# A graph network's last pass: the chunk softmax's pieces put two to a step, and the summing of a group moved from 32 to 26 steps behind its gathers

## What is computed

```
h = x @ W[r];  s = h @ a_src[r];  d = h @ a_dst[r]          # per relation r
e = leaky_relu(s[src] + d[dst], 0.2), only edges of type r and a loop at each node
alpha = exp(e - max over edges with the same dst) / sum of the same
out = x @ W_self + b_self + sum over r of (segment_sum(alpha * h[src]) + bias[r])
```

## Time and profile before

| | us |
|---|---|
| median of 3 runs | 8430.0 (8417.5 to 8430.58) |
| the profiled execution's own time | 8409.43 |
| its span, first to last instruction | 8407.5 |
| POOL busy | 5989.0 (71%) |
| PE busy | 3614.6 (43%) |
| DVE busy | 3113.7 (37%) |
| ACT busy | 1009.6 (12%) |

### The profile page before, as it was taken

One profiled execution on the slowest core, in us unless ns is written; L12 is line 12 of the kernel. 1 busy time (PEld: TensorE's weight loads), 2 busy tenths in 40 slices (PEclk: granted clock), 3 DMA queues, 4 the chain that ended last, 5 costly groups with the idle time before them and its releaser, 6 DMA issues.

```text
span 8407.5 us, 78987 instructions
## 1 busy us (share of the span) xinstructions
PE 3614.6 (43%) x14426; PEld 2885.7 (34%) x14427; DVE 3113.7 (37%) x5678; ACT 1009.6 (12%) x3308; POOL 5989.0 (71%) x6283
## 2 busy tenths in 40 slices
PE   3444333333344434444344343434512555555555
PEld 3333333332222222222222222222312454555555
DVE  3323232323223232323222222222444566666666
ACT  0000000000000000000000000000200233333335
POOL 7777777776777777776777777777267777777770
PEclk6566565555665656566565655656655666666667
DMA  2111111111222222222111111111444554554553
GB/s 58 31 30 30 30 30 30 30 30 42 54 56 57 55 58 55 58 55 48 28 29 28 29 28 29 28 29 28 136 112 102 125 141 128 138 132 129 139 139 86
DMA packets 575401, 546.64 MB, mean 65 GB/s; under 512 B 344667, under 2 KB 344667, under 8 KB 575008
## 3 DMA queue, kind: packets, MB, share of 16 engines
q0 software_dynamic: 200704, 212.34, 13.8%
q1 hardware_dynamic: 345920, 271.71, 11.7%
q10 hardware_dynamic: 28384, 58.61, 1.9%
HBM read 440.61 MB, written 100.74 MB: 64 GB/s over the span
## 4 chain that ended last, share of the span: by engine, by line
POOL 56%; issue 24%; DVE 8%; PE 4%; DVEq 3%; DMA 2%; ACT 1%; POOLq 1%; ACTq 0%; SPq 0%
POOL gat L776 56%; PE p_b L1388 2%; DVEq L331 1%; DMA trip<-in_type_w 1%; ACT msg L989 1%; DVE sel L2031 1%; DVE sel L2035 1%; PE p_a L1449 1%; PE p_a L1447 1%; DVE oh L1668 0%; PE p_all L1377 0%; DVE oht L2027 0%; DVE sum_t L2063 0%; DVE dtab L2128 0%; ACT spare L1036 0%
## 5 line engine op out<-in xcount | busy, mean ns | idle before, releaser
L776 POOL DMA_INDIRECT gat<-x_d,idx x3136 | 2966.3, 946 | 1018.0 <-issue 1018.0
L776 POOL DMA_INDIRECT gat<-rel_d,idx x1568 | 1535.3, 979 | 685.7 <-issue 632.6
L776 POOL DMA_INDIRECT gat<-in_x,idx x1568 | 1485.5, 947 | 486.7 <-issue 486.7
L1668 DVE SCALAR_TENSOR_TENSOR oh<-dstf,fine_col,p_b 128x512 f32<-128x512 f32 x1578 | 1107.3, 743 | 381.9 <-issue 342.5
L1251 PE MATMUL p_all<-oh,gat 128*128 128x256 f32 x1568 | 720.6, 640 | 1194.6 <-DMA gat<-x_d,idx 1153.6
L1251 PE MATMUL p_all<-oh,msg 128*128 128x256 f32 x1568 | 714.5, 635 | 1183.4 <-DVE oh L1668 1183.4
L1237 PE MATMUL p_all<-oh,msg 128*66 128x128 f32 x3136 | 703.1, 417 | 1188.4 <-DVE oh L1668 1188.4
L1237 PEld LDWEIGHTS p_all<-oh,msg 128*66 128x66 f32 x3136 | 637.8, 230 | 1251.7 <-issue 1096.0
L1251 PEld LDWEIGHTS p_all<-oh,gat 128*128 128x128 f32 x1568 | 488.9, 327 | 1423.9 <-issue 1115.5
L1251 PEld LDWEIGHTS p_all<-oh,msg 128*128 128x128 f32 x1568 | 486.1, 325 | 1399.8 <-issue 1080.4
L1388 PE MATMUL p_b<-oh,msg 128*72 128x128 f32 x3136 | 664.7, 400 | 81.5 <-ACT msg L989 35.8
(11 more groups left out here) (275 smaller groups left out, 3344.1 us busy)
## 6 DMA issues: line engine op xcount, KB each, us to landing
he_d<-gat ACTq DMA_DIRECT2D x196, 288.0 KB
ea<-he_d SPq DMA_DIRECT2D x196, 288.0 KB
ea<-in_edge_attr SPq DMA_DIRECT2D x196, 256.0 KB, 2.7
gat<-x_d,idx POOLq DMA_INDIRECT x3136
drow<-dst_d SPq DMA_DIRECT2D x196, 256.0 KB
spare<-rel_d SPq DMA_DIRECT2D x98, 288.0 KB
gat<-in_x,idx POOLq DMA_INDIRECT x1568
gat<-rel_d,idx POOLq DMA_INDIRECT x1568
```

The costliest lines, as they stand in the source:

```text
L776: nc.gpsimd.indirect_dma_start(out=gat[:, q, s, :] if width == HROW else got[:, q, s, :], out_offset=None, in_=table, in_offset=bass.Indir ...
L1668: return vec.scalar_tensor_tensor(out=oh[:, u, cut, :], in0=bc(dst.unsqueeze(2), P, S // 2, W), scalar=fine_col[0:P, bass.ds(at, 1)], in1= ...
```

## The change

LAG goes from 32 to 26, READY from 48 to 46 and LAST from 246 to 244. The pieces of the softmax stand at other steps of the chunk:

| piece | engine | j before | j after |
|---|---|---|---|
| near (loads) | SP | 2 | 0 |
| widen | DVE | 1 | 1 |
| others | DVE | 3 | 2 |
| lay_scores, evict_scores | PE, ACT | 3, 4 | 2, 3 |
| own_scores, lay_self | DVE, PE | 5, 5 | 4, 4 |
| own_self, with_self | DVE | 6 | 5 |
| breaks, most_so_far | DVE | 7, 8 | 6, 6 |
| most_of_all, gaps | DVE | 9, 10 | 7, 7 |
| factors, exponents | DVE, ACT | 11, 11 | 8, 8 |
| sum_so_far, back_exponents | DVE, PE | 12, 12 | 9, 9 |
| sum_of_all, own_sums | DVE | 13, 0 of the next chunk | 10, 10 |
| back_sums | PE | 1 of the next chunk | 11 |
| weights | DVE | 2 of the next chunk, after the look | 12, before the look |
| chunk_shares | DVE | 4 of the next chunk, before the look | 12, before the look |

```diff
-LAG = 2 * CH + 4
+LAG = 2 * CH - 2
-READY = LAG + CH + SETTLE
+READY = LAG + CH + SETTLE + 4
...
-                if j == 2 and CH <= lo < G + CH:
+                if j == 0 and CH <= lo < G + CH:
...
-                    for at, piece in ((4, evict_scores), (11, exponents)):
+                    for at, piece in ((3, evict_scores), (8, exponents)):
...
-                if j == 1 and 2 * CH <= lo < G + 2 * CH:
-                    back_sums(k - 1)
...
-                    for at, piece in ((3, lay_scores), (5, lay_self), (12, back_exponents)):
+                    for at, piece in ((2, lay_scores), (4, lay_self), (9, back_exponents), (11, back_sums)):
...
+                k, j = chunk_of(it, i)
+                if CH <= lo < G + CH and j == LAG - CH:
+                    weights(k)
...
-                    for at_step, piece in ((0, own_sums), (2, weights)):
-                        if j == at_step:
-                            piece(k - 1)
                 if CH <= lo < G + CH:
-                    pieces = {1: (widen,), 3: (others,), 5: (own_scores,), 6: (own_self, with_self), 7: (breaks,),
-                              8: (most_so_far,), 9: (most_of_all,), 10: (gaps,), 11: (factors,), 12: (sum_so_far,),
-                              13: (sum_of_all,)}
+                    pieces = {1: (widen,), 2: (others,), 4: (own_scores,), 5: (own_self, with_self), 6: (breaks, most_so_far),
+                              7: (most_of_all, gaps), 8: (factors,), 9: (sum_so_far,), 10: (sum_of_all, own_sums)}
```

More of the change, by code:

```diff
@@ L2225, in look_share_and_scan @@
                     ahead()
-                k, j = chunk_of(it, i)
-                if 2 * CH <= lo < G + 2 * CH:
-                    for at_step, piece in ((0, own_sums), (2, weights)):
-                        if j == at_step:
-                            piece(k - 1)
                 if CH <= lo < G + CH:
-                    pieces = {1: (widen,), 3: (others,), 5: (own_scores,), 6: (own_self, with_self), 7: (breaks,),
-                              8: (most_so_far,), 9: (most_of_all,), 10: (gaps,), 11: (factors,), 12: (sum_so_far,),
-                              13: (sum_of_all,)}
+                    pieces = {1: (widen,), 2: (others,), 4: (own_scores,), 5: (own_self, with_self), 6: (breaks, most_so_far),
+                              7: (most_of_all, gaps), 8: (factors,), 9: (sum_so_far,), 10: (sum_of_all, own_sums)}
                     for piece in pieces.get(j, ()):
```

## The result

| | before | after |
|---|---|---|
| median of the runs made together, us | 8426.5 (4) | 8478.8 (4), 8476.7 to 8480.4 |
| ratio to before, 95% interval | | 1.0063 [1.0051, 1.0075] |
| span of the profiled execution | 8407.5 | 8474.8 |
| one chunk's round (steps 56 to 168, by 8) | 149.1 | 156.8 |
| last gather to the end | 227.3 | 211.6 |

The change makes the kernel 0.63% slower, 52 us. I had forecast 8450, slower by 0.25%, in the range 8408 to 8482: the direction and both halves of the account came, the size was less than half. The measured time lies only 3 us under the upper end of the range.

What follows compares the result with a forecast made beforehand. Bound by the round of DVE with ACT and PE, not POOL: +4.5 us a chunk, +40 over nine chunks, less chunk 13's slack and a tail of -17, gives +21 us; median 8450, +0.25%, range 8408 to 8482.

Steps and rivals of the forecast that it cites:

- Who sets the pace: Last pass from step 56: the round of DVE with ACT and PE, 149.1 us a chunk, needs longest, not POOL.
- The tail: Behind the last gather, 227.3 us before: six fewer steps, -33 us, +14 given back, 2 off for ACT: -17 us.
- near one step wider: Load used two steps after its issue, not one, so DVE's wait before `others` goes: -1.9 us a chunk.
- The last block's products: PE's products at j = 7 are covered by a scan and `gaps`, shortening DVE's look wait: -2.2 us a chunk.
- lay_scores, +2.5: At j = 2 nothing hides PE's 5.4 us behind `aggregate`, so DVE's next look waits: +2.5 us a chunk.
- back_sums, +3.0: PE's 3.80 us at step 11 has little cover before DVE's `weights`, so DVE waits: +3.0 us a chunk.
- The turned rows, +2.5: ACT's gap moves to j = 12, as long as today, leaving `own_sums` in the open at step 10: +2.5 us a chunk.
- The sum: All terms of a chunk's round together: +4.5 us a chunk, bounds -1 and +8, the middle taken.
- Rival 1: Round as long as before, added waits absorbed, tail's gain kept: -17 us, 8413, faster; chance 0.20.
- 2 (half): About half the round's growth comes, 2 to 2.5 us a chunk: -2 us, 8428, no change; chance 0.24.
- Rival 4: ACT in j = 13 to 2 adds its own, round grows by 8 us: 8480, much slower; chance 0.09.
- rival 3: The forecast itself: additions come as read, 3.5 to 7 us a chunk, 8441 to 8473, 8450 likeliest; chance 0.47.

Runs made afterwards that it cites:

- `near` early: Changed kernel with near's loads issued by SP at j = 11 of the chunk before, not at j = 0: 8458.8 us, 1.0028.
- Late turning: x rows turned at READY + 2, not READY - 6: in the changed kernel 8452.0 us, 1.0018; in the kernel before 8423.6 us, 0.9992.
- the three edits: Changed kernel with near's loads at j = 11, back_sums ahead of the look, and x rows turned at READY + 2; all in one: 8397.9 us, 0.9956.

## Why the prediction was right, and where it fell short

**Who sets the pace.** Right. The round of DVE, ACT and PE bounds the last pass, and POOL's waits grow as it does (53 to 126 us; 90 forecast).

**The tail.** Right: last gather to the end 15.7 us shorter, forecast 17. The parts are each within 4 us of mine: up to step 196 5.5 us longer (2 forecast), from there to the step with the last weights 30.1 shorter (33), the 13 sums 1.1 shorter (0), the rest 10.1 longer (14).

**near one step wider.** The wait before L2084 went, as forecast, and was worth less than the 1.9 us: in the eight chunks it had been 2.0 us in the mean, not the 2.50 of the one step that I had read, and is 0.76 now, so 1.2 us. But the step that set the price of the moved loads counted only who uses them, and not what is issued behind them on SP. This is the step that failed: 4.1 us a chunk, by j = 2 with and without it (3.7 by the round). The order was the same before: there too `near` came ahead of a tile's load, and ACT stood nearly as long, but ACT was done with the tile before the shares of j = 4 were there. The timeline of the kernel before, around:

```profile
7198.48 0.35 SPq L634 DMA_DIRECT2D spare<-rel_d  x1
...
7207.30 2.02 ACT L1036 ACTIVATE spare<-spare,self_w 128x64 f32<-128x64 f32 x8 [9.79 <-DMA spare<-rel_d]
...
7211.35 0.26 ACT L987 ACTIVATE msg<-xt 128x64 f32<-128x64 f32 x1 [2.03 <-DVE xt L2052]
```

ACT's `weigh` waited for the shares 2.03 us more (0.4 to 2.1 in the eight chunks), so the late load cost nothing. The change moved the shares away and left the load uncovered. This last link is read from the two traces and was not tried in a run.

**The last block's products.** Right, with the number: DVE's wait for the look behind them, at j = 10 before and j = 8 now, fell from 3.1 to 0.9 us in the mean, -2.2 as forecast. The timelines of steps 108 (before) and 106 (after):

```profile
7282.20 0.56 DVE L2031 TENSOR_TENSOR sel<-p_all,w_wrt 128x384 f32<-128x384 f32 x1 [4.31 <-PE p_all L1377]
```
```profile
7301.25 0.56 DVE L2029 TENSOR_TENSOR sel<-p_all,w_wrt 128x384 f32<-128x384 f32 x1 [0.73 <-PE p_all L1377]
```

That the new place also keeps them apart from `back_exponents` I had not seen.

**lay_scores, +2.5.** The wait is there, but smaller. At j = 3 DVE waits 0.6 to 2.8 us for the look in the eight chunks, 1.45 in the mean, which is 1.0 above the usual 0.5. Step 101, and the longest, step 157:

```profile
7239.06 1.69 PE L1394 MATMUL p_all<-ident,xs 128*112 128x128 f32 x14
...
7243.89 0.64 PE L1377 MATMUL p_all<-trip_s,oht 128*128 x8
7244.68 0.56 DVE L2029 TENSOR_TENSOR sel<-p_all,w_wrt 128x384 f32<-128x384 f32 x1 [0.97 <-PE p_all L1377]
...
7878.68 0.56 DVE L2029 TENSOR_TENSOR sel<-p_all,w_wrt 128x384 f32<-128x384 f32 x1 [2.80 <-PE p_all L1377]
```

I had reckoned DVE's next look 1.7 us behind `aggregate`; `others`, a tile and the next sum come first, and they cover most of PE's 4.8 us. With `near` early, where DVE no longer stands at j = 2, the mean wait at j = 3 is 1.9 us, so some of this term was hidden behind the one that I had missed.

**back_sums, +3.0.** Right: 21.5 us in 7 waits, 3.1 each, 2.4 more than the gap that stood before `weights` in the kernel before (0.65); removing it gave 2.9 at j = 12 and 2.1 in the round.

**The turned rows, +2.5.** Right in kind, too small. Besides `own_sums` in the open, which no run tried by itself, the gap grew, from 3.65 to 5.80 us of wait for ACT in these steps and from 4.2 to 6.0 in the mean. Late turning took 4.6 us off j = 13, and 3.2 off j = 1 in the kernel before.

**The sum.** With each term at what it measured: +4.5 + 0.7 (the wait for `near`) - 1.5 (`lay_scores`) - 0.6 (`back_sums`) + 1.4 to 1.8 (turned rows) + 3.7 to 4.1 (loads behind `near`) = 8.2 to 9.0, and 7.75 measured, so about 1 us is not placed. The steps up to 56 and the last two chunks added 14 us for which I had 2. The upper bound of all terms, +8, held, by little; I had taken the middle, with `lay_scores` too large in it, the turned rows too small, and a term of 4 us missing. That the time still fell inside the range is partly luck: the range's width came from terms that I had, and what filled it was one that I had not.

**The rivals.** Rival 1 (absorbed) and 2 (half) fell. Rival 4, that ACT with its tiles and loads in j = 13 to 2 adds its own, had 8 us a chunk and 8480, close to the measured 7.75 and 8479, and j = 2 is such a step. (By the forecast's own working 8 us a chunk come to 8486, and the 7 us of rival 3 to 8476 and not 8473.) What it lacked is the reason: the load was late because of what stood ahead of it, and not ACT slow. The forecast's case and rival 4 happened together.

## What to carry to other kernels

When a large load is moved along a queue, look at what is issued behind it there within its landing time, not only at its own user: here a wait of 1.2 us was removed and one of 4.1 us made, and exchanging the order only passed it to the next load. Look too at what the load itself has to wait for, since the queue waits with it. In a schedule written as steps, a piece has no price of its own; it has one for each step, by what the other engines do in that step, and pieces of two independent loops that meet on one engine can cost more than the change at hand (7 us a chunk at j = 10). A loss spread over three waits can be undone wait by wait: each of the three edits gave 0.3 to 0.45%, they added, and with them the change is a gain.

## What the runs showed of the hardware

Of two loads of 504 KB issued by SP 0.4 us apart, the second landed 8.6 us after its issue in the median where a load of 288 KB followed 0.7 us behind, and 6.5 us where it followed some 6 us behind. That load of 288 KB was used 4.8 to 5.7 us after its issue when it stood ahead of the two, and 7.5 to 10.9 us after it behind them; the stored rows, as large, behind them 5.7 to 9.7 us. From the first issue to the landing of all 1296 KB 8.4 to 11.8 us pass, 9.6 in the median, or 139 GB/s, beside what gathers and stores moved. By the Trainium skill ("DMA: Bandwidth & Descriptors", section "Anatomy of one DMA — SWDGE (gpsimd) path"), whose figures are for one DMA on POOL's path and not for SP's queue, the 1296 KB would be there in an estimated 5.0 us; the trace has about twice that, and the measurement decides. ACT loads a table before every root, 1.28 us and then 0.30 us for the root itself, and in the kernel before both stood ahead of the copy that DVE waited for.
